# A gated attention and mixture-of-experts block: two banks for up products, mixing weight applied in place, and new queue orders

## The reference

```
x = x + tanh(g0) * xattn(layernorm(x), ctx)
x = x + tanh(g1) * ffn(layernorm(x))

xattn(a, w): a rounded to fp8 in blocks of 1x128, w in blocks of 128x128
             (each with its own scale, 448 / max|block|), then a @ w.T per batch
ffn(a):  probs = softmax(a @ gate_w.T); the best 4 of 8, weights renormalised
         out = sum_e comb[e] * ((silu(a @ wg[e].T) * (a @ wu[e].T)) @ wd[e].T)
             + sigmoid(a @ shared_gate.T) * ((silu(a @ swg.T) * (a @ swu.T)) @ swd.T)
```

## Time and profile before

| | us |
|---|---|
| median of 3 runs | 207.72 (207.12 to 207.93) |
| the profiled execution | 207.36, of which its span 205.6 |
| TensorE busy | 166.9, 81% of the span |
| VectorE / ScalarE / GpSimd busy | 126.7 / 104.6 / 96.0 |
| mean granted TensorE clock | 0.991 |

### The profile page before, as it was taken

One profiled execution on the slowest core, in us unless ns is written; L12 is line 12 of the kernel. 1 busy time (PEld: TensorE's weight loads), 2 busy tenths in 40 slices (PEclk: granted clock), 3 DMA queues, 4 the chain that ended last, 5 costly groups with the idle time before them and its releaser, 6 DMA issues.

```text
span 205.6 us, 2330 instructions
## 1 busy us (share of the span) xinstructions
PE 166.9 (81%) x742; PEld 124.9 (61%) x742; DVE 126.7 (62%) x271; ACT 104.6 (51%) x231; POOL 96.0 (47%) x103
## 2 busy tenths in 40 slices
PE   0013077799698999799898999997999999999993
PEld 0001035678476667566676788765777777777772
DVE  0748883459975989976686542796245644455452
ACT  2266545674279774156666454441464454544530
POOL 6115431365283589845455353443264575544310
PEclk9999999999999999999999999996999999999999
DMA  5998970000000000000000000020000000000002
GB/s 137 333 399 279 316 246 0 0 5 0 0 0 0 0 2 3 0 2 0 0 3 0 2 0 0 0 105 0 0 0 0 0 3 2 0 0 3 0 0 102
DMA packets 4080, 9.97 MB, mean 49 GB/s; under 512 B 585, under 2 KB 585, under 8 KB 4068
## 3 DMA queue, kind: packets, MB, share of 16 engines
q1 hardware_dynamic: 4068, 9.83, 14.0%
HBM read 8.78 MB, written 1.05 MB: 48 GB/s over the span
## 4 chain that ended last, share of the span: by engine, by line
PE 50%; DVE 23%; ACT 12%; issue 9%; POOL 2%; DMA 2%; DVEq 0%; ACTq 0%
PE bank L943 42%; DVE act L736 4%; DVE silu L726 2%; DMA x<-xs 2%; DVE a_lo L741 2%; DVE xq L624 2%; ACT gu_hi L444 2%; PE bank L997 2%; ACT silu L457 2%; PE bank L958 1%; POOL gu_lo L305 1%; DVE bn L562 1%; DVE gt L695 1%; ACT cw L370 1%; PE bank L904 1%
## 5 line engine op out<-in xcount | busy, mean ns | idle before, releaser
L305 POOL TENSOR_TENSOR gu_lo<-w_raw,gu_hi 128x512 fp32r<-128x512 f32 (+1 forms) x34 | 45.4, 1334 | 62.7 <-ACT gu_hi L444 62.6
L943 PE MATMUL bank<-h_hi,gu_hi 128*128 128x512 f32 x128 | 54.9, 429 | 4.6 <-DVE act L736 3.3
L943 PE MATMUL bank<-h_lo,gu_hi 128*128 128x512 f32 x128 | 50.1, 392 | 0.0
L943 PE MATMUL bank<-h_hi,gu_lo 128*128 128x512 f32 x128 | 50.1, 391 | 0.0
L462 ACT ACTIVATE a_hi<-act 128x512 fp32r<-128x512 f32 (+1 forms) x34 | 21.4, 630 | 45.9 <-DVE act L736 45.9
L741 DVE TENSOR_TENSOR a_lo<-act,a_hi 128x512 fp32r<-128x512 f32 (+1 forms) x34 | 24.5, 720 | 16.4 <-ACT a_hi L462 16.2
L736 DVE TENSOR_TENSOR act<-silu,bank 128x512 f32<-128x512 f32 (+1 forms) x34 | 23.3, 686 | 18.3 <-PE bank L943 14.1
L312 POOL TENSOR_TENSOR d_lo<-w_raw,d_hi 128x256 fp32r<-128x256 f32 (+1 forms) x34 | 26.1, 768 | 15.3 <-ACT d_hi L449 15.3
L943 PEld LDWEIGHTS bank<-h_hi,gu_hi 128*128 128x128 f32 x128 | 24.4, 191 | 12.3 <-DVE act L736 4.2
L457 ACT ACTIVATE silu<-bank 128x512 f32<-128x512 f32 (+1 forms) x34 | 20.1, 590 | 20.4 <-PE bank L943 20.4
L943 PE MATMUL bank<-a_hi,d_hi 128*128 128x512 f32 (+1 forms) x68 | 28.5, 420 | 0.2 <-DVE shared L749 0.2
(11 more groups left out here) (120 smaller groups left out, 186.5 us busy)
## 6 DMA issues: line engine op xcount, KB each, us to landing
w_raw<-w_full SPq DMA_DIRECT2D x16, 384.0 KB, 5.6
...
```

The source lines that it names most:

```text
L305: nc.gpsimd.tensor_tensor(gu_lo[:, slot, 0:cols], w_raw[:, c, 0:cols], gu_hi[:, slot, 0:cols].bitcast(F32), ALU.subtract).then_inc(gu_lo_d ...
L943: last = nc.tensor.matmul(out, w[k][a], x_of[k][b], start=(start and k == 0 and i == 0), stop=(stop and k == blocks - 1 and i == 2))
```

## The change

Banks: up products alternate between two banks, MIX, the logits and the transposed routing weights share one. `gated` multiplies silu by the up bank first, `mixed` then multiplies `act` by MIX in place; mix(n) moves from between gate and up to the end of iteration n, and high_a and low_a of unit n to the iteration of n + 1. Units 0 and 1 (it was unit 0) are both computed in two parts of 256 tokens, into their own gate banks. ctx is loaded by batch, and for batches 0 and 1 it is rounded on VectorE (`round_ctx`) instead of GpSimd. The orders of all five queues are rewritten. The diff, cut to its core:

```diff
-GATE, UP, MIX = bank[0:3]
-SHARED_OUT = (bank[3:5], bank[5:7])
-OUT = bank[3:5]
-BLK = (bank[7], bank[7])
-QT = [bank[i] for i in (5, 6, 5, 6)]
...
-ATT = [[bank[i] for i in ks] for ks in ((2, 3), (4, 7), (7, 5), (6, 5))]
-X1T = [bank[i] for i in (5, 6, 7, 6)]
-Y2T = [bank[i] for i in (2, 4, 7, 5)]
-LOGIT = (bank[3], bank[7])
-LOGIT_T = (bank[5], bank[7])
-COMBT = (bank[6], bank[7])
+GATE, UP, MIX = bank[0], bank[1:3], bank[3]
+GATE_FIRST = (bank[0], bank[6])
+OUT = bank[4:6]
+SHARED_OUT = (bank[4:6], bank[6:8])
+BLK = (bank[3], bank[6])
+QT = [bank[i] for i in (6, 7, 7, 6)]
+ATT = [[bank[i] for i in ks] for ks in ((4, 5), (3, 7), (6, 7), (7, 6))]
+Y2T = [bank[i] for i in (4, 5, 7, 6)]
+X1T = [bank[i] for i in (7, 4, 7, 6)]
+LOGIT = LOGIT_T = COMBT = bank[3]
...
     load_x(0)
     load_ctx(0)
+    load_ctx(1)
+    load_w(0)
     load_x(1)
-    load_w(0)
     sp.dma_start(small_in[:], small).then_inc(small_landed, 16)
     load_w(1)
+    load_x(2)
+    load_ctx(2)
+    load_ctx(3)
+    load_x(3)
+    load_w(2)
     sp.wait_ge(spread_zeroed, 1)
     sp.dma_start(spread[0:3 * G, 0:ROWS], sel).then_inc(sel_landed, 16)
-    load_w(2)
-    load_x(2)
-    load_ctx(1)
-    load_x(3)
...
     inverse_std(0, 0, var_ready, rstd_ready)
+    pool.wait_ge(ctx_diag, 1)
+    low_gu(0)
     inverse_std(0, 1, var_ready, rstd_ready)
-    add_magic(0)
-    subtract_magic(0)
-    add_magic(1)
-    subtract_magic(1)
+    pool.wait_ge(att_ready, 1)
+    low_gu(1)
     inverse_std(1, 0, var1_ready, rstd1_ready)
-    low_gu(0)
     inverse_std(1, 1, var1_ready, rstd1_ready)
-    for n in range(ALL):
-        if n == 1:
...
-            inverse_std(0, 2, var_ready, rstd_ready)
+    inverse_std(0, 2, var_ready, rstd_ready)
+    low_d(0)
+    for n in range(1, ALL):
         if n + 1 < ALL:
             low_gu(n + 1)
-        if n == 4:
+        if n == 1:
...
             inverse_std(0, 3, var_ready, rstd_ready)
+        if n == 8:
+            add_magic(3)
+        if n == 11:
+            inverse_std(1, 2, var1_ready, rstd1_ready)
+        if n == 13:
+            inverse_std(1, 3, var1_ready, rstd1_ready)
+        low_d(n)
         if n == 6:
             add_magic(2)
         if n == 7:
             subtract_magic(2)
-        if n == 8:
-            add_magic(3)
         if n == 9:
             subtract_magic(3)
-        if n == 11:
-            inverse_std(1, 2, var1_ready, rstd1_ready)
-        low_d(n)
-        if n == 12:
-            inverse_std(1, 3, var1_ready, rstd1_ready)
-        if n % UNITS == SHARED_UNITS + 2:
+        if n % UNITS == SHARED_UNITS + 5:
             add_shared(n // UNITS, 0)
-        if n % UNITS == SHARED_UNITS + 3:
+        if n % UNITS == SHARED_UNITS + 8:
             add_shared(n // UNITS, 1)
...
-        nc.scalar.activation(silu[0:rows, slot, :], GATE[0:rows, :], ACT.Silu).then_inc(silu_done, 1)
+        src = GATE_FIRST[n] if n < 2 else GATE
+        nc.scalar.activation(silu[0:rows, slot, :], src[0:rows, :], ACT.Silu).then_inc(silu_done, 1)
...
     centre(0)
+    high_gu(0)
+    scale_x(0)
+    mags_x(0)
     a.wait_ge(small_landed, 16)
     nc.scalar.activation(g_tanh[:], small_in[:, 0:2], ACT.Tanh).then_inc(tanh_done, 1)
-    scale_x(0)
     scale_ctx(0)
-    mags_x(0)
     mags_ctx(0)
     centre(1)
+    copy_xqt(0)
     scale_ctx(1)
-    copy_xqt(0)
+    mags_ctx(1)
     scale_x(1)
-    mags_ctx(1)
     mags_x(1)
+    residual0(0)
+    high_gu(1)
+    copy_xqt(1)
+    norm_x1(0)
+    residual0(1)
+    high_h(0)
     a.wait_ge(gate_zeroed, 1)
     nc.scalar.activation(gate_hi[:, :, 0:GP], small_in[:, 2:].rearrange("p (k g) -> p k g", k=KC), ACT.Copy)\
         .then_inc(gate_hi_done, 1)
-    residual0(0)
-    high_gu(0)
-    copy_xqt(1)
-    residual0(1)
-    norm_x1(0)
-    high_h(0)
+    high_d(0)
     norm_x1(1)
     high_h(1)
-    copy_x1t(0)
-    copy_x1t(1)
     for n in range(ALL):
-        if n + 1 < ALL:
+        if 1 <= n < ALL - 1:
             high_gu(n + 1)
+        if n == 6:
...
+            copy_comb(0)
         silu_unit(n)
-        high_d(n)
+        if n >= 1:
+            high_a(n - 1)
+            high_d(n)
         if n == 0:
+            centre(2)
...
             copy_logits(0)
-            centre(2)
+            copy_x1t(0)
+            copy_x1t(1)
+            centre(3)
...
         if n == 5:
+            scale_ctx(2)
+        if n == 6:
             copy_sg(0)
-            scale_ctx(2)
-            scale_x(2)
-        if n == 6:
             mags_ctx(2)
-            mags_x(2)
+            scale_x(3)
+        if n == 7:
+            mags_x(3)
             scale_ctx(3)
-        if n == 7:
-            scale_x(3)
+            copy_xqt(2)
+        if n == 8:
             mags_ctx(3)
-            mags_x(3)
...
         if n == 9:
-            copy_xqt(2)
+            residual0(2)
         if n == 10:
-            residual0(2)
-        if n == 11:
             copy_xqt(3)
+        if n == 12:
+            residual0(3)
             norm_x1(2)
-        if n == 12:
-            copy_x1t(2)
-            residual0(3)
         if n == 13:
-            high_h(2)
             norm_x1(3)
         if n == 14:
-            copy_x1t(3)
+            high_h(2)
         if n == 15:
             high_h(3)
+        if n == 16:
+            copy_x1t(2)
         if n == UNITS:
+            copy_x1t(3)
             copy_logits(1)
...
-        high_a(n)
+    high_a(ALL - 1)
...
+    def round_ctx(b):
+        flat = "p k n c -> p (k n c)"
+        v.wait_ge(ctx_magic, b + 1)
+        val, mag = cw[:, b].rearrange(flat), cm[:, b].rearrange(flat)
+        after(did(nc.vector.tensor_tensor(val, val, mag, ALU.add)))
+        nc.vector.tensor_tensor(cq[:, b].rearrange("p k c -> p (k c)"), val, mag, ALU.subtract).then_inc(cq_ready[b], 1)
...
+    def gated(n):
+        slot, rows = n % DEEP, rows_of(n)
+        up = GATE[LAST:2 * LAST, :] if is_small(n) else UP[n % 2][:]
+        v.wait_ge(silu_done, n + 1)
+        v.wait_ge(products_done, n + 1)
+        nc.vector.tensor_tensor(act[0:rows, slot, :], silu[0:rows, slot, :], up, ALU.mult).then_inc(gated_done, 1)
     def mixed(n):
         slot = n % DEEP
-        v.wait_ge(silu_done, n + 1)
+        v.wait_ge(gated_done, n + 1)
         v.wait_ge(mix_done, mixes(n) + 1)
-        nc.vector.tensor_tensor(silu[:, slot, :], silu[:, slot, :], MIX[:], ALU.mult).then_inc(mixed_done, 1)
-    def gated(n):
-        slot, rows = n % DEEP, rows_of(n)
-        up = GATE[LAST:2 * LAST, :] if is_small(n) else UP[:]
-        if is_expert(n):
-            v.wait_ge(mixed_done, experts(n) + 1)
-        else:
-            v.wait_ge(silu_done, n + 1)
-        v.wait_ge(products_done, n + 1)
-        nc.vector.tensor_tensor(act[0:rows, slot, :], silu[0:rows, slot, :], up, ALU.mult).then_inc(act_done, 1)
+        nc.vector.tensor_tensor(act[:, slot, :], act[:, slot, :], MIX[:], ALU.mult).then_inc(mixed_done, 1)
...
     stats_x(0)
+    max_ctx(0)
     max_x_0 = max_x(0)
-    max_ctx(0)
+    max_ctx(1)
     scales_x(0, max_x_0)
     v.wait_ge(consts, 1)
+    block_scales_ctx(0)
     stats_x(1)
-    block_scales_ctx(0)
     copy_scales_ctx(0)
     magic_0 = magic_x(0)
+    added_0 = add_x(0, magic_0)
+    round_x(0, added_0)
     magic_ctx(0)
-    added_0 = add_x(0, magic_0)
+    round_ctx(0)
     max_x_1 = max_x(1)
-    round_x(0, added_0)
     scales_x(1, max_x_1)
     dequant_scales(0)
     magic_ctx(1)
+    round_ctx(1)
     magic_1 = magic_x(1)
     added_1 = add_x(1, magic_1)
-    part_0 = residual1(0)
     round_x(1, added_1)
-    residual_sum(0, part_0)
+    residual1(0)
+    residual_sum(0)
     stats_x1(0)
-    part_1 = residual1(1)
+    residual1(1)
     shift_x1(0)
-    residual_sum(1, part_1)
+    residual_sum(1)
     stats_x1(1)
+    low_h(0)
+    shift_x1(1)
     split_gate_w()
-    shift_x1(1)
-    low_h(0)
+    stats_x(2)
     low_h(1)
+    max_ctx(2)
+    max_ctx(3)
     for n in range(ALL):
+        gated(n)
+        if n >= 1:
...
+            low_a(n - 1)
         if n == 0:
-            stats_x(2)
+            stats_x(3)
+        if n == 1:
+            max_x_2 = max_x(2)
+            scales_x(2, max_x_2)
+        if n == 2:
+            routed = route_compare(0)
+            max_x_3 = max_x(3)
         if n == 3:
-            stats_x(3)
+            ranked = route_rank(routed)
+            block_scales_ctx(1)
+        if n == 4:
+            route_weigh(0, ranked)
+            route_split(0)
         if n == 5:
             copy_scales_ctx(1)
-            scales_x(2, max_x_2)
+            scales_x(3, max_x_3)
+            magic_2 = magic_x(2)
+            added_2 = add_x(2, magic_2)
...
         if n == 6:
+            round_x(2, added_2)
             magic_ctx(2)
-            magic_2 = magic_x(2)
         if n == 7:
-            round_x(2, added_2)
+            dequant_scales(1)
+            magic_3 = magic_x(3)
         if n == 8:
+            added_3 = add_x(3, magic_3)
             magic_ctx(3)
-            magic_3 = magic_x(3)
```

(116 more changed lines are left out.)

90 lines of the change are left out of this document (41 added, 49 removed).

## The result

| | before | after |
|---|---|---|
| median, us (runs) | 207.42 (205.28 to 207.93, 4) | 195.03 (193.94 to 196.08, 4) |
| ratio, 95% interval | | 0.9421 (0.9371 to 0.947) |
| profiled execution, its span | 207.36, 205.6 | 193.94, 192.1 |

The forecast was 193.3, range 188.5 to 200.0. Ratios leave out runs over 1.5% above the fastest of their kernel; medians hold all, among them one of 226.06 us, at a granted clock of 0.79, in experiment 3.

The account below looks back on a forecast made before the run. TensorE was taken as busiest, losing time in four stages, mainly waiting for VectorE. Terms of -6.9, -2.8, -3.0 and -1.7 sum to -14.4, taking 207.36 to 192.96; with 0.36 for the median, 193.3 us, range 188.5 to 200.0.

Parts of the forecast that it names:

- Start: Preparation of batches 0 and 1 up to gate(2): gate(2) at 36.9 instead of 44.13, a term of -6.9 us.
- rival A: First hidden-layer matmuls run at half clock after only five warm-ups: +1.7 us, 195.0; chance 0.13.
- VectorE's straight run: Preparation: VectorE works on without waiting, 0.60 us per 512-element operation, so attend(0) starts at 15.2 instead of 19.05.
- Rival C: Start gains half: VectorE's eight two-input operations before gate(2) take 1.05 us each, +3.6, 196.9; chance 0.09.
- Middle: Gate(2) to gate(7), -3.1 us of which -2.8 was taken; gate(7) to gate(17), 0 to 4.6 recovered, -3.0 taken.
- one unit more room for the up bank: Middle stages: up products wait for the product of two units before, over 4 us more room, no longer for mixing.
- the routing's stalls: Gate(2) to gate(7): VectorE's routing delays scale rows by 0.7 us, comb's transposes by 0.4, gate(6) by 0.55.
- low_gu(10) behind add_magic(3): Gate(7) to gate(17): the moved step with least room, about 0.2 us, as add_magic(3) waits before low_d(8).
- Rival B: The middle gives nothing because contention with GpSimd stretches VectorE: +5.8 us, 199.1; chance 0.11.
- End: Gate(17) to the end: 0.6 less waiting for routing, 1.6 from the clock, 0.5 lost at the tail: -1.7 us.
- The tail's added wait: At the very end mixed(33) comes behind gated(33) and low_a(32): +0.5 us.
- Rival D: Slower: mixing last in a unit makes down wait, 0.7 us in each of 22 expert units, 208.4; chance 0.04.

Follow-up runs that it names:

- experiment 3: The changed kernel with one up bank from unit 2 on and mixing first as before, new queue orders kept: 196.39 us.
- experiment 10: The changed kernel with add_magic(3), GpSimd's addition for ctx(3), one unit later, behind low_gu(10): 193.72 us.
- experiment 1: The changed kernel with its second up bank taken away from unit 2 on: 194.93 us.
- experiments 11: The changed kernel with 8 warm-ups, residual0(1) ahead of norm_x1(0), add_magic(3) one unit later and the second half's comb transposes later: 190.42 us.
- experiment 12: The changed kernel with the other edits of experiments 11, its warm-up matmuls back at 5 instead of 8: 192.55 us.
- experiment 8: The changed kernel with eight warm-up matmuls instead of five: 194.11 us.
- experiment 5: The changed kernel with ctx of batches 0 and 1 rounded on GpSimd again: 197.2 us.

## Why the prediction came out 1.7 us low

Of the 1.7 us, 1.0 lies in the profiled execution (forecast 192.96, measured 193.94), nearly all of it in the start. The other 0.7 is the step from that execution to the median, which was 1.1 and not the 0.36 of the forecast.

**Start (-6.9, measured -5.85; by starts -7.2): mis-sized.** Gate(2) stood at 38.28 instead of 36.9, 1.4 late. The first hidden matmul was late by only 0.2, at 27.06 instead of 26.85, because an earlier landing hid two losses; the other 1.2 lie behind it.
- *Clock, +0.7 in this execution, not in the forecast: rival A.* The kernel after runs its first hidden-layer matmuls like this (timeline), and its windows say so:

```profile
28.20 0.41 PE L1002 MATMUL bank<-h_hi,gu_lo 128*128 128x256 f32 x1
28.42 0.41 PE L1001 MATMUL bank<-h_hi,gu_hi 128*128 128x256 f32 x1
...
29.15 1.23 PE L1006 MATMUL bank<-h_lo,gu_hi 128*128 128x256 f32 x4
...
30.82 0.28 PE L1001 MATMUL bank<-h_hi,gu_hi 128*128 128x256 f32 x1
...
31.78 0.60 PE L921 MATMUL bank<-eye,xc 128*128 128x128 f32 x4
```
```profile
28.00:29.00 1.00, 1.00 (x5) 0.75 (x4) 0.93 (x5) 0.00 (x0) 0.42 (x1) 0.50 0.99 390
```
Of the 24 matmuls ahead of the transposes at 31.78, the first 14 started at half speed. Eight of them lie before 29.15, where TensorE waits for `h_lo` of batch 0 in any case; the 16 from there on took 2.63, and 16 at 0.12 would be 1.9. The 1.7 of A came from all 24 at half speed and 0.12 more for each, where the starts are 0.21 apart instead of 0.12, so 0.09 more. Other executions of this start paid more. From the first hidden matmul to silu(2) it took 13.43 in the kernel after, 14.32 in experiment 10, where all 24 ran at half speed, and 16.39 in experiment 1. In the order of experiments 11 and 12, where `h_lo` is there in time, it is 11.66 with 8 warm-ups and 13.15 with 5, so 1.5. To give A only 0.13 was the error. That five warm-ups were too few is shown for that order and not for this one, where eight met the same half speed (experiment 8). The Trainium skill ("TensorE: Matmul & The Clock Gate", Part 1) has the low clock as the default that activity lifts; the trace agrees in that the clock rose at 30.5, behind the dense work.
- *VectorE's straight run, +0.7.* From the scale copy (10.58) to attend(0) it took 4.07 instead of 3.4. `cm` came 0.35 late, and the working took 0.60 from start to start for every two-input operation of 512. The timeline after has 0.73 where the next operation reads what this one wrote, and 0.61 where it does not, and the 0.60 of the earlier trace rows was of the second kind:

```profile
13.08 0.69 DVE L610 TENSOR_TENSOR cw<-cw,cm 128x512 f32<-128x512 f32 x1
13.81 0.69 DVE L611 TENSOR_TENSOR cq<-cw,cm 128x512 bf16<-128x512 f32 x1
14.42 0.68 DVE L615 TENSOR_REDUCE amax_x<-xc 128x4 f32<-128x512 f32 x1
...
19.03 0.69 DVE L642 TENSOR_TENSOR xq<-xc,xm 128x512 bf16<-128x512 f32 x1
```
Rounding is an addition and a subtraction that reads its result. Nowhere in this run is the 1.05 of before, and GpSimd stood idle from 11.5 to 19.6. That is as the rule of the Trainium skill has it ("SBUF — State Buffer", "Who interferes with whom"), and experiment 5 shows the other side, 1.64 beside GpSimd. Rival C did not come.
- *x(0) landed 1.1 us earlier*, by the first statistics, a gain that the forecast did not have. It makes attend(0) at 14.65 look better than the 15.2 forecast: at the landing of before it would stand near 15.75 (experiment 8, with statistics at 4.97, has 15.57). It may be no chance. The first statistics stand at 4.82, 5.06 and 5.39 in the three kernels with the old order of loads, and at 3.86 to 4.97 in the eleven with the new one, nine of them below 4.31. The loads were costed at nothing; no run changes them alone.
- *The rest, about +1.3.* From attend(0) to the first hidden matmul it took 12.4 instead of 11.65 (+0.8). Behind that, `h_lo` was awaited 0.3 longer, and from batch 1's transposes to its first hidden matmul it took 1.37 instead of 1.05 (+0.3); the last stretch took 0.1 less.

In order of time: the scale copy -1.2 (10.58 against 11.8), VectorE's run +0.7, the way to the first hidden matmul +0.8, `h_lo` +0.3, the clock +0.7, batch 1's transposes +0.3, the last stretch -0.1. Within rounding that is the 1.4 by which gate(2) was late. The median is another 1.1 above the profiled run. An execution whose clock rose as late as in experiment 10 would be 0.9 longer, so I take that for the same clock; but only one execution of each kernel has a timeline, so this is argued and not shown. That the median is A's 195.0 to the tenth is in part luck: A has a price of 1.7, and the profiled execution paid 0.7.

**Middle (-2.8 and -3.0, measured -2.9 and -2.7): right size, wrong mechanism.** The step "one unit more room for the up bank" failed: experiment 1 takes the bank away and nothing moves. The orders of the queues, with what else stays in experiment 3, bring 1.5 and 2.7; the place of the mixing brings 1.2, through `mix_shared(0)` alone, and 0.6. Which order edit does it was not separated, and stays open. The size came from setting the stage against the pitch of its matmuls, which holds whatever removes the idle time. Of the routing's stalls, the 0.7 at the scale rows were 0.17, the 0.4 at comb 0.30, the 0.55 at gate(6) 0.41. The place named as having least room, low_gu(10) behind add_magic(3), was the right one, but the 0.2 of room given to it were a wait of 1.15. Rival B did not come. That gate(17) stood at 109.69 and not near 107.5 is half a slip: the prediction's own terms put it at 121.17 - 12.7 = 108.5.

**End (-1.7, measured -2.0).** The second comb waited 1.01 (1.16 by the pitch) where 1.4 was forecast, and the clock behind it stayed at 1.00, where it had been 0.50:

```profile
133.00:134.00 1.00, 1.00 (x6) 0.78 (x6) 0.22 (x1) 0.63 (x2) 0.29 (x1) 1.00 0.00 0
```
The tail's added wait was 0.36 of `a_lo`, forecast 0.5. Rival D did not come: `a_lo` made TensorE wait this once. By its words the prediction named any wait for `a_lo` as a sign of being wrong, and had itself counted 0.5 for this one.

**Costed at nothing.** Splitting unit 1 was indeed nothing. Three warm-ups fewer, listed as free, saved nothing, since TensorE waits for ScalarE and VectorE anyway (the first hidden matmul at 27.55 with 8, at 27.50 with 5); in the order of experiment 12 they were a cost of 2.1.
